# Expert outputs of a decoder layer: from a slot table that is gathered at the end to scatters that add into a token table

## The reference

```
x = layernorm(x + self_attention(x))
x = layernorm(x + cross_attention(x, ctx))
h = x2 + gqa_attention(rope(rms_norm(x2)))          # inside the third block
y = h + moe(rms_norm(h))
x = layernorm(x2 + y)
```

```
logits = x @ router_w + router_b;   topv, topi = top_k(logits, 2)
topw   = softmax(topv)                               # two gates for each token
eo[e]  = (x @ W2[e] + b2[e]) * silu(x @ W1[e] + b1[e]) @ W3[e] + b3[e]
moe(x) = sum over the 2 chosen experts of topw * eo[e]      # 8 experts, hidden size 512
```

## Time and profile before

| | us |
|---|---|
| median of three runs | 258.11 |
| the profiled execution | 257.8 |
| its span | 255.9 |
| PE busy | 183.2 (72%) |
| DVE busy | 182.7 (71%) |
| POOL busy | 119.5 (47%) |
| ACT busy | 118.8 (46%) |

### The profile page before, as it was taken

The page is one execution under the profiler, slowest core; times in us unless marked ns, Lnnn a source line. Parts: engine busy times, 40 slices in busy tenths (PEclk is TensorE's granted clock), DMA queues, the critical chain, the costliest instruction groups (busy, mean ns, idle before and its releaser), DMA issues. The chain is left out here.

```text
span 255.9 us, 7235 instructions
## 1 busy us (share of the span) xinstructions
PE 183.2 (72%) x2412; PEld 161.5 (63%) x2413; DVE 182.7 (71%) x428; ACT 118.8 (46%) x385; POOL 119.5 (47%) x220
## 2 busy tenths in 40 slices
PE   0477999999999998988774421899999999900000
PEld 0365878788887877777563421899998999900000
DVE  6406799999999999989973496277676777705344
ACT  2344868878788777676242110244454544400000
POOL 0315346655688778744225203445453341047771
PEclk9997999999999999999998555599999999975555
DMA  7699900000008000000001000011112232011212
GB/s 229 147 352 385 289 16 4 3 1 5 1 3 235 18 3 3 1 13 14 23 14 31 0 0 21 23 42 41 62 52 50 41 62 41 21 41 51 51 41 82
DMA packets 21337, 16.06 MB, mean 63 GB/s; under 512 B 3032, under 2 KB 18464, under 8 KB 21312
## 3 DMA queue, kind: packets, MB, share of 16 engines
q1 hardware_dynamic: 19248, 12.02, 16.0%
q0 software_dynamic: 1344, 2.76, 5.2%
q10 hardware_dynamic: 720, 0.95, 1.2%
HBM read 11.78 MB, written 3.93 MB: 61 GB/s over the span
## 5 line engine op out<-in xcount | busy, mean ns | idle before, releaser
L476 POOL DMA_INDIRECT early<-xm_scratch,tok_i x26 | 26.3, 1012 | 44.2 <-DMA early<-xm_scratch,tok_i 26.7
L898 DVE TENSOR_REDUCE smax<-score 128x16 f32<-128x1024 f32 x24 | 29.0, 1209 | 11.9 <-PE score L551 11.9
L384 POOL TENSOR_TENSOR k<-kt,cst 128x512 f32<-128x512 f32 x24 | 25.3, 1054 | 16.4 <-ACT kt L772 16.4
L905 DVE TENSOR_TENSOR s_sb<-score,smax 128x1024 f32<-128x1024 f32 x24 | 29.4, 1224 | 1.6 <-PE bank L499 0.8
L782 ACT ACTIVATE pt_sb<-bank 128x512 f32<-128x512 f32 x48 | 26.2, 594 | 9.3 <-PE bank L499 8.8
L551 PE MATMUL score<-k,q 64*128 64x256 f32 x192 | 26.3, 393 | 0.0
L499 PE MATMUL bank<-cst,s_sb 128*128 128x128 f32 x192 | 25.9, 279 | 0.0
L915 DVE RECIPROCAL rsum<-bank 128x128 f32<-128x128 f32 x24 | 22.8, 951 | 2.4 <-PE bank L584 2.4
L499 PEld LDWEIGHTS bank<-cst,s_sb 128*128 128x128 f32 x192 | 22.1, 144 | 0.8 <-issue 0.7
L702 PE MATMUL bank<-w,pt_sb 128*128 x160 | 22.2, 282 | 0.0
L691 PE MATMUL score<-xgt,w_now 128*128 128x128 f32 x160 | 21.4, 291 | 0.4 <-ACT xgt L854 0.4
(11 more groups left out here) (167 smaller groups left out, 383.8 us busy)
## 6 DMA issues: line engine op xcount, KB each, us to landing
w_up<-in_L_ffn_W SPq DMA_DIRECT2D x2, 2048.0 KB, 12.1
w<-in_L_ffn_W SPq DMA_DIRECT2D x8, 256.0 KB, 6.5
y_scratch<-eo SPq DMA_DIRECT2D x1, 1536.0 KB, 7.7
y_scratch<-eo SPq DMA_DIRECT2D x10, 128.0 KB
cst<-in_consts ACTq DMA_DIRECT2D x1, 672.5 KB, 4.2
early<-in_x SPq DMA_DIRECT2D x1, 512.0 KB, 6.0
early<-in_ctx SPq DMA_DIRECT2D x1, 512.0 KB, 4.3
xm_scratch<-xm SPq DMA_DIRECT2D x8, 64.0 KB, 1.5
```

Source lines behind the costliest of these rows:

```text
L384: g.tensor_tensor(k2[:, n % 3, :, :, :], kt[:, n % 2, :].rearrange("c (b u k) -> c b u k", b=2, u=1).to_broadcast([P, 2, NQ, S]), mask_p.r ...
L476: pool.indirect_dma_start(xg[:, j, :], None, xm_d[:, :], bass.IndirectOffsetOnAxis(ap=tok_i[:, j:j + 1], axis=0)).then_inc(g_gather, 16)
L898: v.tensor_reduce(smax[:, :, :], score[:, :, :].rearrange("q b (p k) -> q b p k", k=S), AX.X, ALU.max).then_inc(d_mx, 1)
L905: v.tensor_tensor(s_sb[:, :, :].rearrange("q b (p k) -> q (b p) k", k=S), score[:, :, :].rearrange("q b (p k) -> q (b p) k", k=S), smax[:, ...
```

## The change

The slot table is replaced by a token table. `y_scratch` now has 1024 rows, one for each token, and 128 spare rows. SP first writes `base` into it. Each expert tile leaves PSUM times the gates of its slots. GpSimd then sends the tile with an indirect transfer whose rows go to their tokens' rows and are added there. Slots without a token have rows in the spare part. Since two tiles may hold the same token, each such transfer is issued only when the one before has landed (`g_sc`), so all 20 form one chain. When it is done, SP reads the table back in plain order, and VectorE goes straight to the statistics.

What comes with it:
- The tokens in `tok_i` are counted from 1, and row 0 of `xm_scratch` is zero. `row_i` holds each slot's row of the table.
- The gates of the slots, `g_slot`, come from a product like that for `tok_i`. The gates are split into three bf16 parts (`gate_p`) and spread over `hi_g` (128 x 16 x 3 x 26), and 16 matmuls give the sum.
- The scatters of the first 14 tiles (`SURE` = 7 pairs, which are always in use) are written out between the gathers. The others run in a loop on GpSimd whose count is `last`, with a tiny product `all_in` on each pass.
- `eo` has 13 tiles instead of 24. Tiles from 13 on use two buffers, `eo_last`, so VectorE waits there for the landing of earlier scatters.
- `last_scale` works in three groups of 3, 3 and 2 tiles.

```diff
+SURE = NT - 1
+NE_KEPT = 2 * SURE - 1
...
@@ SyncE @@
             sp.wait_ge(c_zero, 9)
-            sp.dma_start(y_d.rearrange("(a q) e -> q a e", q=P), eo[:, :, :]).then_inc(y_zero, 16)
+            sp.dma_start(xm_d[0:1, :], eo[0:1, 0, :]).then_inc(y_zero, 16)
+            sp.dma_start(y_d[SPARE:SPARE + P, :], eo[:, 0, :]).then_inc(y_zero, 16)
...
+            sp.wait_ge(c_base, NT)
+            sp.dma_start(y_d[0:SPARE, :].rearrange("(t q) e -> q t e", q=P), base[:, :, :]).then_inc(y_zero, 16)
+
             sp.wait_ge(d_ex, 1)
             last = sp.value_load(last_i[0:1, 0:1], min_val=NT - 1, max_val=NJ // 2 - 1)
-            with sp.Fori(0, last + 1) as i:
-                sp.wait_ge(d_eo, 2 * i + 2)
-                sp.dma_start(y_d.rearrange("(a q) e -> q a e", q=P)[:, bass.ds(i * 2, 2), :],
-                             eo[:, bass.ds(i * 2, 2), :]).then_inc(y_out_s, 16)
+            y_row = y_d[0:SPARE, :].rearrange("(t q) e -> q t e", q=P)
+            sp.wait_ge(y_zero, 48)
+            sp.wait_ge(g_sc, last * 32 + 32)
+            for t in range(NT):
+                sp.dma_start(acc[:, t, :], y_row[:, t, :]).then_inc(g_yg[t], 16)
...
@@ GpSimd @@
-            for j in range(NG):
-                pool.indirect_dma_start(xg[:, j, :], None, xm_d[:, :],
-                                        bass.IndirectOffsetOnAxis(ap=tok_i[:, j:j + 1], axis=0)).then_inc(g_gather, 16)
-                if j % 2 == 1:
-                    pool.wait_ge(g_gather, 16 * (j + 1))
-
+            def gather(i):
+                if i >= 1:
+                    pool.wait_ge(g_gather, 32 * i)
+                for j in (2 * i, 2 * i + 1):
+                    pool.indirect_dma_start(xg[:, j, :], None, xm_d[:, :],
+                                            bass.IndirectOffsetOnAxis(ap=tok_i[:, j:j + 1], axis=0)).then_inc(g_gather, 16)
+
+            def scatter(idx, src):
+                pool.indirect_dma_start(y_d[:, :], bass.IndirectOffsetOnAxis(ap=idx, axis=0), src, None,
+                                        compute_op=ALU.add).then_inc(g_sc, 16)
+
+            for i in range(4):
+                gather(i)
+            pool.wait_ge(d_row, 2)
+            pool.wait_ge(y_zero, 48)
+            for i in range(SURE):
+                gather(i + 4)
+                for u in range(2):
+                    j = 2 * i + u
+                    pool.wait_ge(d_eo, j + 1)
+                    if j >= 1:
+                        pool.wait_ge(g_sc, 16 * j)
+                    scatter(row_i[:, j:j + 1], eo[:, j, :] if j < NE_KEPT else eo_last[:, u, :])
+            for i in range(SURE + 4, NG // 2):
+                gather(i)
...
-            for t in range(NT):
-                for k in range(2):
-                    pool.indirect_dma_start(yg[:, 2 * t + k, :], None, y_d[:, :],
-                                            bass.IndirectOffsetOnAxis(ap=slot_i[:, k, t:t + 1], axis=0)).then_inc(g_yg[t], 16)
...
+            with pool.Fori(SURE, last + 1) as i:
+                for u in range(2):
+                    pool.wait_ge(g_sc, 32 * i + 16 * u)
+                    pool.wait_ge(g_all, 2 * i + u + 1 - 2 * SURE)
+                    pool.wait_ge(d_eo, 2 * i + 1 + u)
+                    all_done()
+                    pool.wait_ge(y_zero, 48)
+                    scatter(row_now[:, u:u + 1], eo_last[:, u, :])
...
@@ VectorE @@
+            link(v.tensor_copy(gate_p[:, 0, :], gates))
...
+            v.tensor_tensor(hi_g[:, :, :, :], hi_hot[:, :, :].rearrange("q c (u j) -> q c u j", u=1).to_broadcast(part),
+                            gate_p[:, :, :].rearrange("q r (c u) -> q c r u", u=1).to_broadcast(part),
+                            ALU.mult).then_inc(d_gp, 1)
...
             def keep_out(u, j):
                 v.tensor_scalar(eo[:, bass.ds(j, 1), :].rearrange("q a e -> q (a e)"), ps_e[u][:, 0:D],
-                                0.0, None, ALU.add).then_inc(d_eo, 1)
+                                g_slot[:, bass.ds(j, 1)], None, ALU.mult).then_inc(d_eo, 1)
...
+                if not kept:
+                    dve.wait_ge(g_sc, 32 * i + 16)
+                    last_row(0, 2 * i + 2)
...
-                step(v.scalar_tensor_tensor(acc[:, t, :], yg[:, 2 * t, :], rv[:, 5, t:t + 1], base[:, t, :],
-                                            ALU.mult, ALU.add))
-                step(v.scalar_tensor_tensor(acc[:, t, :], yg[:, 2 * t + 1, :], rv[:, 6, t:t + 1], acc[:, t, :],
-                                            ALU.mult, ALU.add))
...
+            for t in range(NT + 1):
+                if t < NT:
+                    spread(t)
+                if t >= 1:
+                    mean_var(t - 1)
+            normalise(0)
+            for t in range(1, NT):
+                normalise(t)
```

More of the change, by code:

```diff
@@ L56 @@
 C_ORD = C_T + 2 * NT
-C_END = C_ORD + NE
+C_U = C_ORD + NE
+C_END = C_U + 1
+SPARE = NT * P
 def decoder_kernel(nc, t_in, consts, out):
@@ L252, in decoder_kernel @@
         y_zero = sem("y_zero")
-        y_out_s = sem("y_out_s")
+        g_sc = sem("g_sc")
+        d_gate = sem("d_gate")
+        d_gp = sem("d_gp")
+        pe_gate = sem("pe_gate")
+        d_row = sem("d_row")
         g_all = sem("g_all")
@@ L494, in _ @@
+            for k in range(3):
+                last_scale(k, 3 * k, min(3 * k + 3, NT))
         @block.tensor
@@ L675, in _ @@
             k.then_inc(pe_tok, 1)
+            ps_gate = bank[6][:, 0:3 * NG]
+            pe.wait_ge(d_gp, 1)
+            for c in range(2 * NT):
+                k = mm(ps_gate, lo_hot[:, c, :], hi_g[:, c, :, :].rearrange("q r j -> q (r j)"),
+                       start=(c == 0), stop=(c == 2 * NT - 1))
+            k.then_inc(pe_gate, 1)
             ps_h1, ps_h2 = [bank[0], bank[2]], [bank[1], bank[3]]
@@ L735, in _ @@
                 pe.wait_ge(d_eo, 2 * i + 1)
+                pe.wait_ge(d_gate, 1)
                 down(1, before_b, 8 * i + 4)
@@ L1150, in _, with turn_of @@
             keep_out(0, 0)
-            with dve.Fori(0, last) as i:
+            def turn_of(i, kept):
                 ea, eb = pair_of(i + 2)
@@ L1158, in _ @@
                 hidden(0, 8 * i + 8)
+                if not kept:
+                    dve.wait_ge(g_sc, 32 * i)
+                    last_row(1, 2 * i + 1)
                 dve.wait_ge(pe_e, 2 * i + 2)
-                keep_out(1, 2 * i + 1)
+                if kept:
+                    keep_out(1, 2 * i + 1)
+                else:
+                    keep_last(1, 2 * i + 1)
                 dve.wait_ge(d_hh, 8 * i + 12)
@@ L1170, in _ @@
[L1170 to L1176, removed]
-                ins.then_inc(d_st, 1)
-                dve.wait_ge(d_st, fin[0])
+            with dve.Fori(0, SURE - 1) as i:
+                turn_of(i, True)
+            with dve.Fori(SURE - 1, last) as i:
+                turn_of(i, False)
+            dve.wait_ge(g_sc, 32 * last)
+            last_row(1, 2 * last + 1)
+            dve.wait_ge(pe_e, 2 * last + 2)
+            keep_last(1, 2 * last + 1)
@@ L1183, in normalise @@
                                 ALU.subtract, ALU.mult).then_inc(d_fin, 1)
-            dve.wait_ge(c_base, NT)
-            for t in range(NT):
-                if t == NT - 1:
-                    for n in range(NT // 2):
-                        normalise(n)
-                dve.wait_ge(g_yg[t], 32)
-                step(v.scalar_tensor_tensor(acc[:, t, :], yg[:, 2 * t, :], rv[:, 5, t:t + 1], base[:, t, :],
-                                            ALU.mult, ALU.add))
-                step(v.scalar_tensor_tensor(acc[:, t, :], yg[:, 2 * t + 1, :], rv[:, 6, t:t + 1], acc[:, t, :],
-                                            ALU.mult, ALU.add))
-                step(v.bn_stats(fstats[:, t, :], acc[:, t, :]))
-                v.bn_aggr(fmv[:, t, :], fstats[:, t, :]).then_inc(d_fmv, 1)
@@ L1197, in _ @@
-            for n in range(NT // 2, NT):
-                normalise(n)
+            for t in range(NT + 1):
[6 more added lines that the diff above has]
+                normalise(t)
 def _consts():
```

72 lines of the change are left out of this document (55 added, 17 removed).

## The result

| | before | after |
|---|---|---|
| median of four runs each, us | 257.88 (257.36 to 258.13) | 282.65 (281.88 to 284.18) |
| profiled execution, us | 257.8 | 281.88 |
| its span, us | 255.9 | 279.7 |
| GpSimd busy | 119.5 (47%) | 140.5 (50%) |

After / before is 1.097 (95% interval 1.092 to 1.102). The change makes the kernel 9.7% slower: 24.8 us by the medians. The forecast was 271 in a range of 258 to 286. Single executions that fell into a slower state are left out of the ratios that have an interval, but not out of the medians in us.

A forecast was written before the change was run, and what follows sets the result against it. GpSimd's chain of scatter landings was to replace TensorE as the bound: a 16 us gain in the tail against a 29 us loss in the chain. Span 269.2 plus 1.9 gave 271.1 us, in general 226.9 + 13c; range 258 to 286.

The forecast's parts named there:

- L: Time from the start of scatter 0 to the start of scatter 19; the forecast had 78.0 us.
- c: Time from one scatter's start to the next one's when only the landing is waited for; taken as 3.4 us.
- two legs: Rival: an add reads old rows, then writes them, so c is 4.3 and both scatters bind; 285 us, chance 0.16.
- Start: Kernel start: smaller clearing of `eo` allowed -0.3 us; fifth gather pair at 172.8.
- Gates: VectorE ahead of `load_up`: five small operations and one product add 2.5 us, which GpSimd hides.
- Six rounds: GpSimd's expert loop: six rounds of 3.93 + 3.4 us, 44.0 in all, to 216.8.
- The four late gathers: Two last pairs, for empty slots, stand ahead of scatter 14 on GpSimd, which starts at 233.4.
- Five more: Last GpSimd loop: five more scatters at c + 0.6 us, 20.0 in all; scatter 19 starts at 253.4.
- port lock: Rival: VectorE copies hold shared ports, delaying GpSimd by 0.725 us in each of 13 scatters; +9, 280 us, chance 0.05.
- Tail: After scatter 19 lands: loads, statistics, normalising and stores take 12.6 us to the end.
- fast landing: Rival: an add lands like the smallest stores, c is 2.3; 256.8 us, not slower than before, chance 0.14.
- Half clock: Rival: TensorE idles ahead of tile 17, then runs at 1.2 GHz; +4, 275 us, chance 0.07.

The follow-up runs named there:

- run 5: The changed kernel run again unaltered, on the same chip as two other variants: 1.107 times the kernel before, 283.37 us.
- run 7: The kernel before, with the clearing of `eo` moved behind the copies of the first weights: 0.999 times the kernel before.
- Run 1: The changed kernel with its 20 scatters as plain stores, the add left out and every wait kept: 1.033 times the kernel before, 264.38 us.
- experiment 2: The changed kernel without the last four gathers (slot tiles 22 to 25, empty with these inputs): 1.080 times the kernel before, 278.54 us.
- 3: The changed kernel with all gathers kept, one behind each scatter instead of two behind each second: 1.077 times the kernel before, 275.47 us.
- run 6: The changed kernel with two token tables (even and odd tiles) and without the gathers of empty slot tiles: 0.991 times the kernel before, 253.98 us.
- 4: The changed kernel with even and odd tiles added into two tables, each scatter waiting for the one before the last: 1.024 times the kernel before, 261.9 us.

## Why the prediction was right, and what was mis-sized
The mechanism was right: one chain of landings on GpSimd replaces TensorE as the bound, and costs more than the tail it removes. The size came out 10.5 us of span too small (269.2 forecast, 279.7 measured), more than all of it in L. The measured 282.65 lies in the wide range, but outside the forecast's own of 261 to 278, and c lies outside the 2.65 to 3.93 that it stood for. Both are nearer to the *two legs* rival (c = 4.3, 285). By the prediction's own steps:

1. *Start.* The fifth pair at 172.14 (172.8 forecast), scatter 0 at 175.09 (175.4). That is luck in part: the trace happened to have the earlier front, and in run 5 scatter 0 starts at 177.83. The clearing is worth nothing (run 7).
2. *Gates.* I had 2.5 on VectorE. What counts is the time from the first gather to the first slots taken. It rose from 4.30 (155.57 to 159.87) to 5.52 (153.36 to 158.88): 1.2. VectorE's timeline after:
```profile
154.85 0.23 DVE L1153 TENSOR_TENSOR rv<-rv 128x8 f32<-128x8 f32 x1
...
156.29 1.46 DVE L1161 TENSOR_TENSOR hi_g<-hi_hot,gate_p 128x1248 bf16<-128x1248 f32 x1
157.66 1.30 DVE L1183 COPY w_now<-w_up 128x1032 f32 x2
158.88 0.41 DVE L1180 TENSOR_SCALAR xs<-early 128x256 f32<-128x256 f32 x1
```
The product is 1.46 (1.4 forecast). But before, 1.1 us stood idle between the row of 157.06 in the earlier trace rows and the first weight copy; now no idle shows there, since the wait runs beside the product. GpSimd hid all of it, as forecast.
3. *Six rounds*, 52.8 against 44.0. **c was the mis-sized term**, 4.12 instead of 3.4. In the 12 landing-bound steps of L that is +8.6. The second half of the miss in this step is the issue, which the sum took at a gather's 1.01: an adding scatter takes 1.6 to 2.0 on the engine. So GpSimd needs 4.67 of its own behind each odd scatter, not 3.93: 6 x 0.74 = +4.4. Both halves have one source. The forecast's 3.4 was a gather's issue of 0.95 and 2.45 behind it. Measured ahead of the odd scatters are an issue of 1.66 (mean) and 2.46 behind it. **What the sum lacked is the longer issue of an adding scatter, 0.7 us.** That the 2.46 agrees is luck. The sum made it up of 1.6 to the landing, 0.26 from there to the next start and 0.6 for a second leg in DRAM. From the chain of waits:
```profile
192.81 3.31 DMA y_scratch<-eo,row_i
...
196.89 1.96 POOL y_scratch L502
```
The landing comes 1.69 behind the issue of 1.62, where a gather's took 1.6, so only 0.1 of the 0.6 is there. But from the landing at 196.12 to the next scatter's start there are 0.77. Run 1's plain scatters have the same 0.77 (203.27 + 2.28 = 205.55, next at 206.32), and land 1.28 behind their issue. So against a plain store the add costs 0.63 in the issue and some 0.4 in the landing (that may be a second leg; no run separates it), and the delay of 0.77 belongs to any scatter behind a wait here. What GpSimd does in it no run shows. The *two legs* rival had c nearly right (4.3), but in the main for another reason, and without its consequence. It had both scatters of a round bound by landings; the longer issue leaves GpSimd no idle time behind the odd one, because 4.67 is above 4.12.
4. *The four late gathers*, 10.92 against 10.6. Right, and experiments 2 and 3 show that most of it (6.2 in experiment 2) goes when no gathers stand there. VectorE stood from about 223 on in the forecast; its timeline has the stall:
```profile
226.86 0.15 DVE L1201 COPY row_now<-row_i 128x1 int32 x1 [13.39 <-DMA y_scratch<-eo,row_i]
...
246.29 0.15 DVE L1201 COPY row_now<-row_i 128x1 int32 x1 [8.15 <-DMA y_scratch<-eo_last,row_now]
```
The second ends with scatter 14's landing (242.91 + 3.25 = 246.16), as forecast. The first is one that I didn't have: VectorE had its 13 kept tiles out by 207.6, and from 213.5 it waited 13.39 for scatter 11 to land. It costs nothing, since the chain runs on meanwhile.
5. *Five more*, 4.33 each against 4.0. With c at 4.12, the loop adds 0.2, not 0.6: the tiny product and the registers lie between landing and next start, which is 0.86 to 0.90 instead of 0.77, and some landings are longer (*port lock*, below). That is -2.0 of L. The sum of steps 3 to 5 is 8.6 + 4.4 + 0.3 - 2.0 = 11.3 of the 11.5 missing.
6. *Tail*, 11.8 against 12.6.

The *fast landing* rival is dead: even a plain scatter has c at 3.05, above its deciding 2.4. *Half clock* happened (3.78 and 3.62) and cost the chain nothing, as weighed. *Port lock* is there, smaller than its 0.7 a step. Scatters beside one of VectorE's weight copies issue in 1.83 to 2.00 instead of 1.55 to 1.74, and their landing comes later by as much: in the last loop the three with a copy beside them land after 3.54 to 3.59, the other three after 3.25 to 3.34, and the steps behind the three are 4.40 to 4.49 where the other two are 4.15 and 4.16. Run 5's trace has the same three and three (3.47 to 3.60 and 3.21 to 3.28). At 247.06 the copy (246.78 to 247.48) reaches 0.42 into the scatter, which takes some 0.3 longer. So the lock costs the chain about 0.3 a time there, some 2 us in all (an estimate: three steps of the loop, and some 0.3 in each of three odd steps of the rounds). No run takes the copies away.

From the Trainium skill's price ("DMA: Bandwidth & Descriptors", "Anatomy of one DMA — SWDGE (gpsimd) path") the prediction had estimated c as 3.36, by counting the 2.15 that follow from that price from the end of the issue. That section of the Trainium skill counts set-up and completion together. Run 1's plain scatter lands 1.28 behind its issue, but 2.28 from its start, near the 2.15. The adding scatter needs 3.3 from its start, and a formula with the bytes alone doesn't tell the two kinds apart.

Bringing the gain home needed both edits of run 6. The expected 16 us of tail were real; a chain that waits for landings, the adding issue and the gathers of empty tiles ate them.

## What to carry to other kernels
Before a tail of issues is traded for work inside a loop, count what one engine must do per round, issues and landing waits both, and compare it with the round of the engine that bounds it. Here a chain of transfers that each wait for the one before cost 4.1 a step, although the DMA engines were about 20% busy; two chains in turn into two targets hid the landings for the price of one addition a tile and a second read. And where an engine's list is in fixed order, put independent issues singly into the waits, not in pairs behind every second one: here that alone was 5 to 7 us.

## What the runs showed of the hardware
- An adding indirect scatter of 128 rows of 512 B is 144 packets, a plain one 32. Its issue occupies GpSimd 1.63 against 1.00 us, and it lands 3.3 after its start against 2.3. Behind a landing that it waits for, either kind starts 0.77 later in the rounds; the one gather that the chain of waits before shows, 0.26 later.
- The waits behind pairs of gathers for empty slots, whose rows are all the same, were long: 3.04 (before 3.03 and 3.36, experiments 1 and 4: 2.99 and 3.38). Behind pairs that hold tokens they were 1.70 to 2.82 before and 1.78 to 3.13 after. So the two kinds overlap, and whether the equal rows are the cause wasn't tested.
- The front of the kernel, nearly the same code in all versions, ends anywhere from 153.4 to 156.1 (the first gather) from kernel to kernel. The granted clock in stretches of 4 us between 19 and 27 us was 0.66 to 0.91 in some of them and full in others, and the two don't go together: with a full clock the first gather came at 153.4 and at 155.8. What sets it stays open.
- A kernel without the tiny product in GpSimd's last loop wasn't tried, so its share of the 4.33 is only argued.
